# Second self attention by masked score matrices, shared feed forward and third self attention in one pipeline, two stages reordered

## The reference

```python
# second self attention (L1_attn), 16 heads of 8
q, k, v = ...                                    # x @ Wproj + bproj
Z = einsum('bhsd,de->bhse', k, W0)
dz1 = vjp1(y1 - v)[0]                            # gradient of a layer norm of Z
KK = mask * einsum('bhtd,bhsd->bhts', k, k)      # mask: lower triangle
Z2 = Z - einsum('bhts,bhsd->bhtd', KK, dz1)
dz2 = vjp2(y2 - v)[0]
A = mask * einsum('bhtd,bhsd->bhts', q, k)
ctx = einsum('bhsd,de->bhse', q, W0) - einsum('bhts,bhsd->bhtd', A, dz1 + dz2)
# then a norm over each head's rows and columns, and ctx @ Wout + bout
# second feed forward (L1_ffn): 64 experts of 64 slots, six for each row, and a shared part
y = zeros.at[tok].add(contrib * wf)
z = silu(xf @ ws1.T) * (xf @ ws3.T) @ ws2.T      # x + y + z
# third self attention (L2_attn)
q, k = relu(q) + EPS, relu(k) + EPS
kv = einsum('bnd,bne->bde', k, v)
z = 1 / (einsum('bnd,bd->bn', q, k.sum(1)) + EPS)
attn = einsum('bnd,bde,bn->bne', q, kv, z)       # @ W_out + b_out
```

## Time and profile before

| | |
|---|---|
| median of three runs | 4386.25 us (4383.8 to 4393.79) |
| the profiled execution | 4399.44 us, span 4397.5 us |
| busy in the span | PE 3267.4 us (74%), PEld 2394.5 (54%), DVE 2842.7 (65%), ACT 1802.4 (41%), POOL 681.8 (16%) |
| mean granted TensorE clock | 0.817 of 2.4 GHz |
| PE, all slices | 3668379366654886755777876999899997786887 |
| DVE, all slices | 6556633499995876174898263555467775556997 |
| TensorE clock, all slices | 9789589666666665577788685999999998998999 |

### The profile page before, as it was taken

How to read it: one execution, slowest core, us unless ns; L and a number is a source line. 1 busy time by engine, 2 the same in 40 slices (tenths; PEclk the granted TensorE clock), 3 DMA queues, 4 the chain that set the end, 5 groups by cost and what they waited for, 6 DMA issues and landing times. The chain is left out here.

```text
span 4397.5 us, 70729 instructions
## 1 busy us (share of the span) xinstructions
PE 3267.4 (74%) x22305; PEld 2394.5 (54%) x22369; DVE 2842.7 (65%) x8231; ACT 1802.4 (41%) x5188; POOL 681.8 (16%) x867
## 2 busy tenths in 40 slices
PE   3668379366654886755777876999899997786887
PEld 3546269222222664534454754666577775554777
DVE  6556633499995876174898263555467775556997
ACT  1346334111112664212777233222155553435886
POOL 0045533100002777200000120000100000000000
PEclk9789589666666665577788685999999998998999
DMA  4040168200004000420300011333200000000000
GB/s 116 1 166 0 33 195 234 73 0 0 0 0 154 3 0 1 126 95 18 74 0 0 1 38 34 103 100 99 86 1 0 0 0 4 0 0 15 1 0 19
DMA packets 135723, 196.88 MB, mean 45 GB/s; under 512 B 24858, under 2 KB 90840, under 8 KB 133846
## 3 DMA queue, kind: packets, MB, share of 16 engines
q1 hardware_dynamic: 124078, 186.31, 14.0%
q0 software_dynamic: 11520, 9.05, 0.7%
HBM read 151.49 MB, written 58.63 MB: 48 GB/s over the span
## 5 line engine op out<-in xcount | busy, mean ns | idle before, releaser
L1260 PE MATMUL l_attn_p_s<-l_attn_outer,l_attn_upper 128*128 128x512 f32 x256 | 204.5, 973 | 113.9 <-DVE l_attn_outer L1203 100.0
L95 POOL TENSOR_TENSOR rstd<-vareps,minus_half 128x32 f32<-128x32 f32 x11 | 59.9, 5444 | 1391.7 <-DVE vareps L86 1258.0
L2583 ACT ACTIVATE l_ffn_sg<-l_ffn_p_g 128x512 f32<-128x512 f32 x168 | 100.3, 597 | 355.4 <-PE l_ffn_p_g L2620 355.4
L2554 DVE TENSOR_TENSOR l_ffn_part<-l_ffn_sg,l_ffn_share 128x512 f32<-128x512 f32 x168 | 116.3, 693 | 190.8 <-ACT l_ffn_sg L2583 183.3
L2610 PEld LDWEIGHTS l_ffn_p_o<-l_ffn_wd,l_ffn_h 128*128 128x128 f32 x1344 | 175.7, 191 | 85.2 <-issue 76.1
L1418 POOL DMA_INDIRECT slots_in<-l_xattn_x,l_xattn_slot x192 | 190.3, 991 | 83.8 <-issue 49.9
L1260 PEld LDWEIGHTS l_attn_p_s<-l_attn_outer,l_attn_upper 128*128 128x128 f32 x256 | 79.2, 324 | 218.7 <-issue 174.4
L2730 ACT ACTIVATE l_attn_E<-l_attn_p_s,l_attn_nm 128x128 f32<-128x128 f32 x512 | 181.2, 386 | 2.9 <-DVE l_attn_nm L2688 2.9
L2610 PE MATMUL l_ffn_p_o<-l_ffn_wd,l_ffn_h 128*128 128x128 f32 x1344 | 178.1, 275 | 2.3 <-DVE l_ffn_h L2557 1.6
L2620 PE MATMUL l_ffn_p_g<-l_ffn_f_xTall,l_ffn_wg 128*128 (+1 forms) x336 | 173.7, 599 | 0.5 <-DVE l_ffn_turned L2545 0.5
L2622 PE MATMUL l_ffn_p_u<-l_ffn_f_xTall,l_ffn_wu 128*128 (+1 forms) x336 | 172.5, 595 | 0.0
(11 more groups left out here) (806 smaller groups left out, 9436.5 us busy)
## 6 DMA issues: line engine op xcount, KB each, us to landing
l_experts_w<-in_L_ffn_w SPq DMA_DIRECT2D x72, 512.0 KB
l_ffn_share<-share_rows SPq DMA_DIRECT2D x112, 256.0 KB, 3.2
slots_in<-l_xattn_empty SPq DMA_DIRECT2D x8, 2145.0 KB, 24.0
shares_out<-l_xattn_zero SPq DMA_DIRECT2D x24, 512.0 KB, 11.5
l_combine_got<-shares_out SPq DMA_DIRECT2D x16, 768.0 KB, 4.5
l_attn_toep<-kernel_rows SPq DMA_DIRECT2D x1, 8192.0 KB, 31.1
xattn_toep<-ssm_rows SPq DMA_DIRECT2D x1, 8192.0 KB
l_slots_w<-in_L_ffn_w SPq DMA_DIRECT2D x32, 176.0 KB
```

The lines of the kernel that those rows point to most:

```text
L1260: mm = pe.matmul(p_s[:, r, a], upper[:], outer[:, r, a * 512:(a + 1) * 512], start=True, stop=True)
L2554: dve.tensor_tensor(part[:, w], sg[:, w], share[:, slot], ALU.mult).then_inc(s.share_used, 1)
L2583: act.activation(sg[:, k], p_g[:, k], ACT.Silu).then_inc(s.silu_ready, 1)
```

## The change

**l1_attn.** The running states go. For each sequence PE makes the score matrices k·k and q·k of all 16 heads, 128 by 128 each (`scored`: 16 matmuls on strips of 32 rows, four strips side by side), into `p_s`. DVE multiplies the first by the triangle into `keys`; ACT copies the second into `queries`, and POOL multiplies that by the triangle in place. `applied` then takes each head's masked matrix as stationary operand, 128 by 128, and that head's 8 columns of dz as moving operand: 16 matmuls for each matrix. DVE takes the results from PSUM. Keys and queries are now made with features on the partitions (`kq`, and `kTm`, four copies of the keys with other heads' rows zeroed, by ACT); `proj` keeps three parts. The depth is 4.

**l1_slots.** Four buffers in place of two, DMAs four steps ahead, and one step to a turn with the blocks of neighbouring steps between each other, written out.

**l1_out** takes the place of l1_combine and l2_attn: for each pair the shared feed forward, the six routed rows (three added by POOL, three by PE through an identity into the same PSUM as the down projection), the norm (POOL for two columns), and the attention, in one pipeline of depth 4 with no barrier inside.

**l3_xattn.** On PE, L2952 and L2956 stand behind L2961, and L2952 writes to another bank (`p_c`). On DVE the keys' product (L2872) goes ahead of the addition to x, and the statistics of x to the end.

```diff
 def l1_attn(nc, R, A):
...
-                for item in skewed(pool, 3, PAIRS):
-                    for b, u in item(2):
+                for item in skewed(pool, 4, PAIRS):
+                    for b, u in item(1):
+                        for r in range(2):
+                            pool.wait_ge(s.scores2_read, b * 2 + (r + 1))
+                            pool.tensor_tensor(queries[:, u % 2, r], queries[:, u % 2, r], causal, ALU.mult).then_inc(s.queries_ready, 1)
...
-                    for b, u in item(2):
-                        applied(s.states2_psum, b, s.part2_read, part2, q_[u], step2[:])
-                        chain(dve.tensor_tensor(qw[u], qw[u], step2[:], ALU.subtract))
+                    for b, u in item(3):
+                        dve.wait_ge(s.step2_psum, b * 2 + 2)
+                        chain(dve.tensor_tensor(qw[u], qw[u], p_w[:, 0:W], ALU.subtract))
                         dve.tensor_reduce(gs[:, 0], heads(qw[u]), AX.X, ALU.add).then_inc(s.sums_ready, 1)
...
+                    for b, u in item(0):
                         for r in range(2):
-                            dve.tensor_tensor(square(outer2[:, r]), over_columns(k_[u][:, r * P:(r + 1) * P]),
-                                              over_rows(dz2[:, r * P:(r + 1) * P]), ALU.mult).then_inc(s.outer2_ready, 1)
...
+                            dve.wait_ge(s.scores1_psum, b * 2 + (r + 1))
+                            dve.tensor_tensor(keys[:, r], scores, causal, ALU.mult).then_inc(s.keys_ready, 1)
...
+                def copied(b, u, r):
+                    act.wait_ge(s.scores2_psum, b * 2 + (r + 1))
+                    act.activation(queries[:, u % 2, r], scores, ACT.Copy).then_inc(s.scores2_read, 1)
...
+                        for c in range(2):
+                            act.activation(kq[:, u % 2, c], p_y[:, c * W:(c + 1) * W], ACT.Identity, bias=bqk[:, c:c + 1])
+                        for m in range(SUB):
+                            last = act.activation(kTm[:, u % 2, :, m], side(p_y[:, 0:W]), ACT.Identity, scale=head4[:, m:m + 1], bias=bhead[:, m:m + 1])
...
-                def states(b, r, ready, psum, outer):
-                    pe.wait_ge(ready, b * 2 + (r + 1))
-                    for a in range(2):
-                        mm = pe.matmul(p_s[:, r, a], upper[:], outer[:, r, a * 512:(a + 1) * 512], start=True, stop=True)
...
+                def scored(u, r, c):
+                    for m in range(SUB):
+                        for j in range(4):
+                            rows = slice(32 * j, 32 * j + 32)
+                            mm = pe.matmul(p_s[:, j, m * P:(m + 1) * P], kTm[rows, u % 2, r, m], kq[rows, u % 2, c, r * P:(r + 1) * P], start=True, stop=True)
+                    return mm
+
+                def applied(out, a, r, dz):
+                    for h in range(H):
+                        mm = pe.matmul(out[:, r * P + h * HD:r * P + (h + 1) * HD], a[:, h], dz[:, r * P + h * HD:r * P + (h + 1) * HD], start=True, stop=True)
+                    return mm
...
 def l1_slots(nc, R, A, xb, ys):
...
-                with pe.Fori(0, NP // W) as i:
+                for item in written_out(2, NP, V):
...
-def l1_combine(nc, R, A, ys, xTall):
...
+def l1_out(nc, R, A, ys, xTall):
...
+                    for b, u in item(0):
+                        pool.wait_ge(got_in[u], (b // V + 1) * DMA)
+                        for n in range(SPLIT):
+                            add = pool.tensor_tensor(pair(R.x, b), pair(R.x, b), got[:, u, :, n], ALU.add)
...
+                    for b, u in item(1):
+                        pool.wait_ge(s.var_ready, b + 1)
+                        pool.tensor_tensor(rs[:, u % 2], ve[:, u % 2], R.minus_half[:, 0:2], ALU.pow).then_inc(s.rstd_ready, 1)
...
 def l3_xattn(nc, R, A):
...
-                    for b, u in item(4):
-                        pe.matmul(p_r[:, 0], headsT[:], wo[:], start=True, stop=True).then_inc(s.out_psum, 1)
                     for b, u in item(2):
                         pe.wait_ge(s.shift_spread, b + 1)
-                    for b, u in item(1):
-                        pe.matmul(p_c[:, 0:SC], wkv[:, 0:P], cT[:, u % 2], start=True, stop=True).then_inc(s.kT_psum, 1)
-                    for b, u in item(2):
                         for m in range(SUB):
...
                         mm.then_inc(s.shifted_psum, 1)
+                    for b, u in item(4):
+                        pe.matmul(p_c[:, 256:384], headsT[:], wo[:], start=True, stop=True).then_inc(s.out_psum, 1)
+                    for b, u in item(1):
+                        pe.matmul(p_c[:, 0:SC], wkv[:, 0:P], cT[:, u % 2], start=True, stop=True).then_inc(s.kT_psum, 1)
```

More of the change, by code:

```diff
@@ L1181, in _ @@
+                    for b, u in item(4):
                         dve.wait_ge(s.xb_ready, b + 1)
                         dve.wait_ge(s.out_psum, b + 1)
-                        dve.tensor_tensor(pair(R.x, b), side(xb[:]), side(p_o[:, 0:W]), ALU.add).then_inc(s.out_taken, 1)
+                        dve.tensor_tensor(pair(R.x, b), side(xb[:]), side(p_z[:, W:2 * W]), ALU.add).then_inc(s.out_taken, 1)
                         dve.wait_ge(s.out_taken, b + 1)
@@ L1293, in _ @@
                         mm.then_inc(s.ctxT_psum, 1)
+                    for b, u in item(3):
+                        pe.wait_ge(s.squares_ready, b + 1)
+                        pe.matmul(p_w[:, W + 2 * H:W + 4 * H], R.ones[:], gs[:, 1], start=True, stop=True).then_inc(s.sqmean_psum, 1)
                     for b, u in item(1):
-                        for r in range(2):
-                            after(pe, s.part2_read, b * 2 + (r - 1))
-                            states(b, r, s.outer1_ready, s.states1_psum, outer1)
+                        pe.wait_ge(s.scores2_read, b * 2 + 1)
+                        scored(u, 1, 1).then_inc(s.scores2_psum, 1)
@@ new lines, in _ @@
+                    for b, u in item(1):
+                        pe.wait_ge(s.dz1_ready, b + 1)
+                        for c, _ in item(4):
+                            pe.wait_ge(s.out_taken, c + 1)
+                        for r in range(2):
+                            applied(p_z, keys[:, r], r, dz1[:, u % 2]).then_inc(s.step1_psum, 1)
+                    for b, u in item(0):
+                        for c, _ in item(1):
+                            pe.wait_ge(s.scores2_read, c * 2 + 2)
+                        scored(u, 0, 0).then_inc(s.scores1_psum, 1)
@@ L1298, in _ @@
                     for b, u in item(2):
[L1299 to L1301 removed]
+                        pe.wait_ge(s.dz2_ready, b + 1)
+                        pe.wait_ge(s.queries_ready, b * 2 + 2)
+                        applied(p_w, queries[:, u % 2, 0], 0, dz2).then_inc(s.step2_psum, 1)
                     for b, u in item(0):
[L1303 removed]
@@ L1304, in _ @@
-                        projected(b, 0)
-                        projected(b, 1)
-                    for b, u in item(3):
-                        pe.wait_ge(s.ctxT_ready, b + 1)
-                        after(pe, s.out_taken, b)
-                        for r in range(2):
-                            mm = pe.matmul(p_o[:, r * P:(r + 1) * P], cT[:, r * P:(r + 1) * P], wout[:], start=True, stop=True)
-                        mm.then_inc(s.out_psum, 1)
+                        pe.wait_ge(s.keys_ready, b * 2 + 1)
```

633 lines of the change are left out of this document (324 added, 309 removed).

## The result

The kernel after takes 4574.48 us (median of four runs, 4570.97 to 4580.07) beside 4386.69 for the kernel before in the same comparison: a ratio of 1.0427, with a 95% interval of 1.0409 to 1.0445. It is slower, as forecast, but by 188 us instead of 80, and 24 us outside the range.

A forecast was written before the change was run, and what follows sets the result against it. DVE bounded l1_attn and PE would after the change, at 1.2 GHz in the bursts. l1_attn +168, l1_out -66, l3_xattn -20 and l1_slots -2 gave +80 us on 4386: 4466 us, range 4355 to 4550.

The forecast's parts named there:

- The bound moves from DVE to PE: l1_attn: DVE falls from 28.2 to 18.5 us a pair, PE needs 43.3 and becomes the bound; stage +168 us.
- both signs: l1_attn: PE busy over 90% of the stretch, and DVE busy near 300 us and waiting for PE.
- The price of a record in the bursts: l1_attn: 128 records a pair at 0.2125 us each, clock 1.2 GHz, 27.2 us a pair, some 437 us in all.
- Rival (a): l1_attn's bursts run at 2.4 GHz: turn about 27.5 us, stage -46 us, kernel 4252 us; chance 0.10.
- Rival (b): l1_attn: the clock falls only some way into each burst; turn 34 us, stage +62, kernel 4360 us; chance 0.10.
- POOL's masks "under PE's turn": l1_attn: POOL's two masks, 11.6 us at most, lie under PE's turn; what waits for them comes over a burst later.
- The waits of 1 us and the relief of 3 us from the high clock: l1_attn: PE waits about 1 us for DVE at turn start; work at 2.4 GHz saves 3 us; turn 41 us.
- The ends, 105 us: l1_attn: the short turns at both ends, with 2 pairs' work and unhidden latencies, take about 105 us.
- rival (c): Waits add up: l1_attn's turn 44 us, l1_out only -9 us, l3_xattn -10; kernel 4578 us; chance 0.13.
- l1_out, -66: l1_combine and l2_attn merged into l1_out: 7.8 us a turn at the high clock, 154 us, so 66 us less.
- l3_xattn, -20: l3_xattn: moving L2952 and L2956 saves 0.64 us in each of 31 turns, 20 us; turn 7.9 us for 8.6.
- l1_slots, -2 (at most -4): l1_slots: PE does the same instructions and idles only 4.3 us in the stage, so 2 us less, at most 4.

The follow-up runs named there:

- masks_later: Kernel after, with one more wait on POOL so that its masks of a pair's queries begin only when DVE has finished the other pair's dz2: 4488.2 us, ratio 1.0233.
- wide: Kernel after, with each of the same 64 burst matmuls moving up to 128 columns, later heads overwriting what is theirs: 4365.1 us, ratio 0.9943.
- wide_later_order2: Kernel after with bursts of up to 128 columns, POOL's masks behind DVE's dz2, ACT's list reordered, PE's transposes ahead of the means' matmul: 4274.7 us, ratio 0.9730.
- dve_masks: Kernel after, with DVE masking the queries' scores straight from PSUM, without ACT's copies and POOL's masks: 4572.5 us, ratio 1.0419.
- pool_reads: Kernel before, with two idle POOL multiplications of 2048 numbers added to each turn of l1_attn: 4462.3 us, ratio 1.0148.

## Why the prediction was right or wrong

**The bound moves from DVE to PE: right, with one reservation.** PE is busy 84% of the time between 862 and 1640 us, where over 90% was named as the sign, and DVE is busy 433 us in the stage, where 300 was named. In masks_later PE is busy 93% of a turn and DVE 313 us, so both signs were missed through the step that failed, below.

**The price of a record in the bursts: right.** 444 us for 437. That loads set the pace at a given clock, and that so few columns leave the clock at 1.2 GHz, was read from L2393 and L283, and wide shows the second directly: nothing but the moving columns was changed, and the clock rose. Rival (a) had the size about right for that case (27.5 us a turn; 28.0 on average in wide_later_order2, with the waits repaired too), and its condition wrong: a burst without gaps isn't enough here. Rival (b) came true in a small part: in masks_later the head of the first burst runs at 2.4 GHz, but the two later bursts, with strips ahead of each, keep 7.00 us as in the kernel after. The Trainium skill's "TensorE: Matmul & The Clock Gate", Part 1: The HAM clock gate, speaks of sustained activity. If a busy PE is read as activity, by that sentence of the Trainium skill the clock should have risen in the 13.79 us of the first burst. The trace disagrees for 8 moving columns (granted clock 0.50 to its end), and agrees for the burst of up to 128 in wide (0.50 at its head, 0.86 over the rest).

**POOL's masks "under PE's turn": this is the step that failed.** The working asked how long the masks take (11.6 us at most, measured 2 x 4.59) and who waits for their result, and found nobody. It did not ask what they stop while they run. They stop DVE's operations with two operands in SBUF, on the chain to the output's addition, for which the first burst waits. With the masks moved (masks_later) the turn is 42.2 us on average, for 41 forecast; without that it is 48.6. The difference is 4.2 us of waiting and 2.2 of clock lost through it. In the stage it is 93 of the 135 us that l1_attn was above its forecast, and the kernel takes 4488 us, inside the range. The sentence that nothing but a burst later waits for the masks was true, and beside the point. The earlier trace rows gave POOL's price; no row of before shows POOL at work beside DVE in this stage for more than 0.73 us.

**The waits of 1 us and the relief of 3 us from the high clock: both too small, and in masks_later they nearly cancel.** There the average turn has 25.4 us of bursts (for 27.2), 7.3 of strips (for 8.3) and 6.2 of the rest (for 7.8), which is 4.4 us of relief, and 3.0 us of waits: 0.9 for DVE's sum, as forecast, and 2.1 for ACT's copies, which the working took only as a limit to the relief. That the sum came within 1.2 us of the turn is partly luck. The missing pause is also what the relief in the first burst hung on, and the working did not see it.

**The ends, 105 us: too low**, by 25 us in masks_later and 29 in the kernel after; with 14 x 1.2 us for the turns the 25 are what is left of the miss. The second turn already holds the first burst and the third all three, at full length; the sum gave the short turns two pairs' work and about 20 us more. No run looked at this by itself. The sum for a turn of 44 us has a slip: 14 x 44 + 105 - 511.5 is 209.5 and not 213, so rival (c) comes to 4575.

**l1_out, -66: mechanism right, gain undersized.** The stage is 88 us shorter. PE's turn is 7.2 us, and PE is busy in all of it at a clock of 1.00, so the 7.1 us of PE's own work were the turn. The 0.7 us a turn added for the chain did not come, and the ends took 16 us where 29 were counted. Timeline, from one turn to the next:

```profile
2204.66 1.46 PE L2032 MATMUL l_out_p_d<-l_out_got,ident 128*128 128x256 f32 x6
...
2211.83 1.46 PE L2032 MATMUL l_out_p_d<-l_out_got,ident 128*128 128x256 f32 x6
```

**l3_xattn, -20: right**, 25 us. The wait for ACT went from 1.50 us to 1.02, and the turn is 7.73 us, for 7.9 forecast:

```profile
4004.16 1.09 PE L2959 MATMUL l_xattn_p_s<-l_xattn_kTm,l_xattn_qT 32*128 32x480 f32 x8 [1.02 <-ACT l_xattn_E L2947]
...
4011.89 1.09 PE L2959 MATMUL l_xattn_p_s<-l_xattn_kTm,l_xattn_qT 32*128 32x480 f32 x8 [1.02 <-ACT l_xattn_E L2947]
```

**l1_slots, -2 (at most -4): -5.5.** PE's busy time fell too, from 73.0 to 70.1 us for the same instructions at the same clock. The loop is now written out, but what saved the 3 us wasn't tried. A small miss.

**Rival (c)** named nearly the right total, 4578, and by luck: it had l1_out and l3_xattn gain 19 us where they gained 113, and a turn of 44 us where it was 48.6. A total that agrees shows nothing of the terms.

## What to carry to other kernels

Before work is called hidden on GpSimd, look for VectorE's operations with two operands in SBUF, and its copies from SBUF, in the same stretch. Here each stood still until the GpSimd operation ended, up to 4.7 us, whoever needed its result, and a wait that moves the GpSimd work into VectorE's idle time can make the kernel faster. A burst of matmuls that only loads weights and moves a few columns is worth trying with more of them if the result allows: here it cost nothing at a given clock, and most of the bursts then ran at 2.4 instead of 1.2 GHz. When a gap on TensorE is removed, look at the durations and waits behind it before counting the gain: in dve_masks much of it was lost to the clock, and in the two runs with ACT's list reordered more than half came back as another wait.

## What the runs showed of the hardware

- A POOL multiplication of 2048 numbers a row takes 4.5 to 4.7 us with a result and one operand in the same tile, and 3.60 us with both operands the same broadcast triangle (pool_reads).
- DVE's instructions that last longer under it: operations with two inputs in SBUF (0.43 us becomes 4.4 to 4.7) and a copy from SBUF to SBUF (0.17 us becomes 3.36). Reductions stay at 0.42. The wait ends within 0.3 us of the end of POOL's operation, in each of the rows shown.
- A float32 record with 128 stationary columns takes 0.213 us at 1.2 GHz and 0.112 us at 2.4 GHz, start to start, with 8 moving columns (masks_later) as well as with 128 (wide).
- With 8 moving columns the granted clock stays at 0.50 through 13.8 us in which PE is never idle (kernel after); with up to 128 in the same matmuls it goes to 1.00 (wide).
- With the same instructions on PE and waits of 0.6 to 1.7 us between them, output and projection run at 1.2 GHz in dve_masks and at 2.4 GHz in masks_later. What decides it was not found.
